# Conv weights spread by two engines, and chunk 0 quantised ahead of the expert maxima

## The reference, cut to what matters

```python
def fake_quant_nvfp4(t):              # blocks of 16 contiguous elements
    amax = jnp.max(jnp.abs(v), axis=-1, keepdims=True)
    exp = jnp.ceil(jnp.log2(jnp.maximum(amax, 1e-30) / 6.0))
    scale = jnp.where(amax > 0, jnp.exp2(exp), 1.0)
    u = v / scale
    idx = jnp.digitize(jnp.abs(u), mids)      # mids 0.25 0.75 1.25 1.75 2.5 3.5 5.0
    q = jnp.sign(u) * grid[idx]               # grid 0 0.5 1 1.5 2 3 4 6
    return (q * scale).reshape(shape)
...
x = x + conv3x3(fake_quant_nvfp4(_ln_c(x)), fake_quant_nvfp4(L0_conv_w))
t = _to_tokens(x)                     # x: (32, 64, 16, 16)
t = t + moe(_ln_t(t))                 # 8 experts 64->128->64, gelu, top-2 gates
x = _from_tokens(t, x)
```

## Time and profile before

| | us |
|---|---|
| median of 3 runs | 196.88 |
| the runs | 195.55, 196.88, 197.39 |
| profiled execution, its own time | 198.83 |
| its span in the trace | 195.9 |
| PE busy | 166.7 (85%) |
| DVE busy | 138.3 (71%) |
| POOL busy | 127.9 (65%) |
| ACT busy | 116.7 (60%) |

### The profile page before, as it was taken

How to read it: one execution, slowest core, us unless ns; L and a number is a source line. 1 busy time by engine, 2 the same in 40 slices (tenths; PEclk the granted TensorE clock), 3 DMA queues, 4 the chain that set the end, 5 groups by cost and what they waited for, 6 DMA issues and landing times.

```text
span 195.9 us, 3972 instructions
## 1 busy us (share of the span) xinstructions
PE 166.7 (85%) x1214; PEld 84.6 (43%) x1214; DVE 138.3 (71%) x442; ACT 116.7 (60%) x153; POOL 127.9 (65%) x120
## 2 busy tenths in 40 slices
PE   1986159899773697997999999999999899999980
PEld 1984125465472343542443443444443344444420
DVE  0899999999778985794684784595694395344451
ACT  3276902572488283469776767766776656776630
POOL 7699134799980442457577677577668477588482
PEclk9999859999997579999999999999999999999998
DMA  6990000000000059499089379569469559669601
GB/s 163 326 134 0 3 0 2 3 0 3 0 0 0 10 161 206 77 215 199 17 204 206 83 168 208 117 169 207 116 158 201 133 149 208 136 159 204 172 0 54
DMA packets 16320, 22.39 MB, mean 114 GB/s; under 512 B 2344, under 2 KB 8112, under 8 KB 16304
## 3 DMA queue, kind: packets, MB, share of 16 engines
q1 hardware_dynamic: 16144, 22.04, 50.3%
q10 hardware_dynamic: 160, 0.15, 0.3%
HBM read 19.82 MB, written 2.36 MB: 113 GB/s over the span
## 4 chain that ended last, share of the span: by engine, by line
PE 48%; DVE 25%; DMA 11%; ACT 7%; issue 6%; SPq 1%; POOLq 1%; ACTq 0%; DVEq 0%
PE ps L1060 23%; PE ps L1077 21%; DMA gbc<-gate_rows 6%; DVE xn L721 5%; DVE ssum L629 4%; DVE xn L641 2%; DMA gate_rows<-gateT 2%; DVE gbc L703 2%; DMA cw<-in_conv_w 2%; ACT xn L458 2%; DVE gbc L708 1%; DVE gbc L713 1%; PE ps L1016 1%; ACT hl L504 1%; DVE topi L801 1%
## 5 line engine op out<-in xcount | busy, mean ns | idle before, releaser
L411 POOL TENSOR_TENSOR x<-x,y_sb 128x512 f32 (+1 forms) x63 | 80.3, 1274 | 40.7 <-DVE y_sb L840 36.5
L557 ACT ACTIVATE work<-ps,bias_sb,w_back 128x1024 f32<-128x1024 f32 x64 | 77.0, 1204 | 37.9 <-PE ps L1060 37.7
L840 DVE SCALAR_TENSOR_TENSOR y_sb<-ps,bias_sb,gbc 128x512 f32<-128x512 f32 x64 | 47.4, 746 | 41.4 <-PE ps L1077 29.6
L1077 PE MATMUL ps<-work,w_sb 128*64 128x512 f32 x256 | 65.7, 593 | 1.0 <-DVE y_sb L840 0.9
L1060 PE MATMUL ps<-xT,w_hi 128*64 128x512 f16 x256 | 39.6, 389 | 1.1 <-ACT work L557 1.1
L1060 PE MATMUL ps<-xT,w_lo 128*64 128x512 f16 x256 | 39.3, 387 | 0.0
L1060 PEld LDWEIGHTS ps<-xT,w_hi 128*64 128x64 f16 x256 | 13.7, 111 | 33.3 <-issue 30.5
L1077 PEld LDWEIGHTS ps<-work,w_sb 128*64 128x64 f32 x256 | 17.9, 137 | 14.1 <-issue 2.1
L1060 PEld LDWEIGHTS ps<-xT,w_lo 128*64 128x64 f16 x256 | 15.0, 112 | 13.5 <-issue 1.0
L983 PE MATMUL ps<-qpad,cw_bd 128*128 128x512 bf16 x72 | 19.0, 411 | 1.7 <-POOL qpad L355 1.6
L355 POOL TENSOR_TENSOR qpad<-work,xn 128x512 bf16<-128x512 f32 (+1 forms) x8 | 10.6, 1328 | 8.7 <-DVE work L727 8.7
(11 more groups left out here) (113 smaller groups left out, 175.8 us busy)
## 6 DMA issues: line engine op xcount, KB each, us to landing
gbc<-gate_rows SPq DMA_DIRECT2D x16, 768.0 KB, 10.1
gbc<-gate_rows SPq DMA_DIRECT2D x16, 256.0 KB, 4.0
x_sb<-in_x SPq DMA_DIRECT2D x8, 256.0 KB, 5.3
out<-x SPq DMA_DIRECT2D x8, 256.0 KB, 10.4
w_raw<-in_W SPq DMA_DIRECT2D x2, 256.0 KB, 6.5
w_sb<-in_W SPq DMA_DIRECT2D x1, 256.0 KB
gate_rows<-gateT SPq DMA_DIRECT2D x8, 32.0 KB, 3.8
cw<-in_conv_w ACTq DMA_DIRECT2D x2, 72.0 KB, 3.9
```

Of the source, the lines that this page charges most:

```text
L411: pool.tensor_tensor(x2[:, ds(c * W, W)], x2[:, ds(c * W, W)], y_sb[:, u % H_RING, :], ALU.add).then_inc(added, 1)
L557: act.activation(h_sb[:, u % H_RING, :], bank(H + 2 * (u % 2), 2 * W), ACT.Gelu, bias=b1_sb[:, u:u + 1], scale=w_back[:, u:u + 1]).then_in ...
L840: dve.scalar_tensor_tensor(y_sb[:, u % H_RING, :], bank(Y + u % 2), b2_sb[:, u:u + 1], gbc[:, slot, u, :], ALU.add, ALU.mult).then_inc(wei ...
L1077: last = pe.matmul(ps[r * CH:(r + 1) * CH, (Y + u % 2) * W:(Y + u % 2 + 1) * W], w2_sb[:, u, :], h_sb[:, u % H_RING, r * W:(r + 1) * W], s ...
```

## The change

It has four parts.

- The four comparisons on POOL lose their second ALU step (a multiplication by 1.0). POOL's multiplication by the block scale goes away; DVE multiplies the sign by the block scale instead, early, behind a new link on the sign. POOL's last multiplication waits for that (`cw_signed_scale`).
- `cw_x` is written by one copy on DVE (partitions 0 to 63) and one on ACT (64 to 127), each of twice the elements, in place of four on DVE. `cw_bd` is written by ACT (0 to 63) and DVE (64 to 127), in place of two copies on ACT. DVE's copy waits for the matmuls and for ACT's `bias_ready`. ACT's absolute value of chunk 2 moves behind its normalisation of chunk 7 and its new copy.
- DVE does the conv weights and the whole of chunk 0 ahead of the maxima of the expert weights; chunk 1's maxima come behind those.
- PE's transpose of the expert maxima and the matmul that spreads them move behind convolution 0.

```diff
@@ POOL
-                last = pool.tensor_scalar(cw_steps[:, k, :], cw_a[:, :], E2M1_MIDS[k], 1.0, ALU.is_ge, ALU.mult)
+                last = pool.tensor_scalar(cw_steps[:, k, :], cw_a[:, :], E2M1_MIDS[k], None, ALU.is_ge)
...
-            link(pool.tensor_tensor(cw_steps[:, 1, :].rearrange("p (b k) -> p b k", k=BLK),
-                                    cw_steps[:, 0, :].rearrange("p (b k) -> p b k", k=BLK),
-                                    cw_scale[:, :].unsqueeze(2).to_broadcast([128, WBLK, BLK]), ALU.mult))
-            pool.tensor_tensor(cw_n[:, :], cw_steps[:, 1, :], cw_sign[:, :], ALU.mult).then_inc(cw_level_ready, 1)
+            pool.wait_ge(cw_signed_scale, 1)
+            pool.tensor_tensor(cw_n[:, :], cw_steps[:, 0, :], cw_sign[:, :], ALU.mult).then_inc(cw_level_ready, 1)
@@ ACT
             normalise(NCH - 2)
-            take_v(2)
             normalise(NCH - 1)
-            for c in range(3, NCH - 3):
+            act.wait_ge(cw_level_ready, 1)
+            act.wait_ge(cwx_zero, 1)
+            act.activation(cw_x[CH:128, :, :, 1, :], cw_n[CH:128, :].rearrange("p (i k) -> p k i", k=TAPS)
+                           .unsqueeze(2).to_broadcast([CH, TAPS, 2, HALF_IN]), ACT.Copy).then_inc(cwx_by_act, 1)
+            for c in range(2, NCH - 3):
                 take_v(c)
-            act.wait_ge(bT_ready, 1)
             act.wait_ge(cwT_ready, 1)
             act.activation(bias_sb[:, :], ps[:, BT:BT + 2 * EXPERTS], ACT.Copy).then_inc(bias_ready, 1)
-
-            act.wait_ge(cwT_ready, 1)
-            act.wait_ge(cwx_zero, 1)
-            for r in range(2):
-                lanes = slice(r * CH, (r + 1) * CH)
-                last = act.activation(cw_bd[lanes, :, r, :],
-                                      ps[lanes, CWT:CWT + TAPS * CH].rearrange("p (k o) -> p k o", k=TAPS), ACT.Copy)
-                last.then_inc(cwbd_ready, 1)
+            act.activation(cw_bd[0:CH, :, 0, :],
+                           ps[0:CH, CWT:CWT + TAPS * CH].rearrange("p (k o) -> p k o", k=TAPS),
+                           ACT.Copy).then_inc(cwbd_by_act, 1)
@@ DVE
-            dve.tensor_scalar(cw_sign[:, :].bitcast(i32), cw_u[:, :].bitcast(i32), SIGN_BIT, ONE_BITS,
-                              ALU.bitwise_and, ALU.bitwise_or)
+            link(dve.tensor_scalar(cw_sign[:, :].bitcast(i32), cw_u[:, :].bitcast(i32), SIGN_BIT, ONE_BITS,
+                                   ALU.bitwise_and, ALU.bitwise_or))
+            dve.tensor_tensor(blocks(cw_sign), blocks(cw_sign), wide(cw_scale), ALU.mult).then_inc(cw_signed_scale, 1)
...
-                for half in range(2):
-                    lanes = slice(half * CH, (half + 1) * CH)
-                    for r in range(2):
-                        last = dve.tensor_copy(cw_x[lanes, :, r, half, :],
-                                               cw_n[lanes, :].rearrange("p (i k) -> p k i", k=TAPS))
-                last.then_inc(cwx_ready, 1)
+                dve.tensor_copy(cw_x[0:CH, :, :, 0, :], cw_n[0:CH, :].rearrange("p (i k) -> p k i", k=TAPS)
+                                .unsqueeze(2).to_broadcast([CH, TAPS, 2, HALF_IN])).then_inc(cwx_by_dve, 1)
+
+            def take_conv_weights():
+
+                dve.wait_ge(cwT_ready, 1)
+                dve.wait_ge(bias_ready, 1)
+                dve.tensor_copy(cw_bd[CH:128, :, 1, :],
+                                ps[CH:128, CWT:CWT + TAPS * CH].rearrange("p (k o) -> p k o", k=TAPS)
+                                ).then_inc(cwbd_by_dve, 1)
...
             def quantise_step(c):
                 block_bounds(c)
-                if c > 0:
+                if c > 1:
                     bias(c - 1)
...
+            conv_weights()
+            block_maxima(0)
+            block_bounds(0)
+            block_magics(0)
+            magics(0)
+            bias(0)
+            take_conv_weights()
             weight_maxima()
-            block_maxima(0)
-            conv_weights()
-            quantise_step(0)
+            block_maxima(1)
             weight_exponents()
             quantise_step(1)
             weight_powers()
@@ PE
-            pe.wait_ge(xn1_ready, XN_BY_DVE)
-            pe.wait_ge(w_amax_ready, 1)
-            pe.transpose(ps[0:EXPERTS + 1, WT:WT + 128], w_amax[:, :], identf[:, :]).then_inc(w_maxT_ready, 1)
...
             for c in range(NCH):
                 convolve(c)
+                if c == 0:
+                    pe.wait_ge(xn1_ready, XN_BY_DVE)
+                    pe.wait_ge(w_amax_ready, 1)
+                    pe.transpose(ps[0:EXPERTS + 1, WT:WT + 128], w_amax[:, :], identf[:, :]).then_inc(w_maxT_ready, 1)
+                    pe.wait_ge(w_diag_ready, 1)
+                    pe.matmul(ps[:, WB:WB + EXPERTS + 1], ones_row[:, :], w_diag[:, :],
+                              start=True, stop=True).then_inc(w_spread, 1)
```

More of the change, by code:

```diff
@@ L167, in program @@
         cw_steps_ready = sem("cw_steps_ready")
+        cw_signed_scale = sem("cw_signed_scale")
         cw_level_ready = sem("cw_level_ready")
-        cwx_ready = sem("cwx_ready")
+        cwx_by_dve = sem("cwx_by_dve")
+        cwx_by_act = sem("cwx_by_act")
         cwT_ready = sem("cwT_ready")
-        cwbd_ready = sem("cwbd_ready")
+        cwbd_by_dve = sem("cwbd_by_dve")
+        cwbd_by_act = sem("cwbd_by_act")
         bT_ready = sem("bT_ready")
@@ L380, in _ @@
             pool.wait_ge(w_hi_ready, 1)
-            pool.wait_ge(cwx_ready, 1)
+            pool.wait_ge(cwx_by_dve, 1)
+            pool.wait_ge(cwx_by_act, 1)
             pool.tensor_tensor(w_scaled[:, 0:NW].rearrange("p (e h) -> p e h", e=EXPERTS),
@@ L965, in _ @@
             last.then_inc(bT_ready, 1)
-            pe.wait_ge(cwx_ready, 1)
+            pe.wait_ge(cwx_by_dve, 1)
+            pe.wait_ge(cwx_by_act, 1)
             for k in range(TAPS):
@@ L971, in _ @@
             last.then_inc(cwT_ready, 1)
[L972 to L976, removed]
+            pe.wait_ge(cwbd_by_dve, 1)
+            pe.wait_ge(cwbd_by_act, 1)
             pe.wait_ge(bias_ready, 1)
```

## The result

The changed kernel takes 201.53 us (median of 4 runs, 199.77 to 204.8) against 197.13 for the kernel before (median of 4, 195.55 to 197.92). The ratio is 1.016, interval 1.009 to 1.023, that is 3.1 us slower (1.8 to 4.5). The medians hold every run and the ratio leaves out the disturbed ones, which is why the one says 4.4 and the other 3.1. The profiled execution took 200.13 with a span of 198.3 (before: 198.83 and 195.9).

The account below looks back on a forecast made before the run. DVE, without gaps in the quantisation, was taken to bound the part before the experts. The walk gave +3.8 at chunk 7 and +4.0 at ACT's L511, taken as +3.9 on the median 196.88: 200.8 us, range 198.0 to 203.0.

Parts of the forecast that it names:

- DVE bounds the first part: Up to chunk 7's bias at 46.73, each us added to DVE or stood still there moves everything behind it.
- Part 1: POOL's cheaper levels: ready between 17.1 and 19.7, before DVE asks at 19.85, so nobody starts earlier; 0 us.
- Part 2: DVE's new multiplication of sign by block scale, beside POOL's first comparison: everything comes 0.75 later, bounds 0.50 and 1.5.
- Rival B: New multiplication on DVE blocked for POOL's whole operation: 1.5 instead of 0.75, total 201.6; chance 0.10.
- Part 3: Chunk 0 first, with one spread copy on DVE at pitch 0.62; chunk 0's bias ends at 23.0 instead of 25.54.
- Part 4: DVE idles 1.3 before its cw_bd copy, for ACT's bias_ready, and 2.35 before the exponents, for PE's transpose behind convolution 0.
- rival A: PE's clock still high at 25.1: convolution 0 takes 2.19, second wait 0.85, walk +2.2, total 199.1; chance 0.17.
- The walk: Step-by-step schedule of chunks 1 to 7: delay of +4.0 at chunk 1, +3.8 at chunk 7, +4.0 at ACT's L511.
- The rule for who waits for POOL: DVE's L708, L713 and L721 wait for a running POOL tensor operation, L721 then needs 0.55 more; others don't wait.
- Rival C: DVE's standing time paid back in the quantisation, six avoided POOL meetings giving 3.3: +0.6, 197.5; chance 0.10.
- Rival D: Convolutions and POOL's first residual set the pace, so convolution 0's 2.0 earlier start reaches the end: 194.9; chance 0.08.

Follow-up runs that it names:

- e1: Changed kernel with ACT's three absolute values (chunks 2 to 4) moved behind its copies of the biases and of cw_bd; 1.023 of the kernel before.
- e4: Kernel before with only the new levels: single-step comparisons on POOL, DVE multiplying the sign by the block scale; 1.0015 of the kernel before.
- e5: Changed kernel with expert maxima ahead of DVE's cw_bd copy, exponents right behind it, PE's transpose and spread ahead of convolution 0; 1.0005 of before.
- e2: Changed kernel with DVE's exponents behind chunk 1's quantisation step and the powers behind chunk 1's bias; 1.021 of the kernel before.
- e11: Changed kernel, ACT's absolute values behind the bias copy, POOL's residuals of chunks 0 to 4 cut to 8 columns; chunk 7's bias at 47.60.
- e9: Kernel before with POOL's residual additions of chunks 0 to 4 cut from 512 to 8 columns; chunk 7's bias at 42.79 instead of 46.73.
- e3: Changed kernel with the old levels: two-step comparisons and block scale on POOL, no sign multiplication on DVE; 203.77 us (200.18 to 206.79).
- e6: Changed kernel, expert transpose and spread before convolution 0, expert then chunk 1 maxima before exponents, both cw_bd halves on ACT; 196.98 us, 0.9946 of before.

## Why the prediction was right

It said 200.8 (198.0 to 203.0), slower; 201.53 was measured. Step by step:

- **DVE bounds the first part** (what bounds the kernel now): right up to chunk 3, where shifts of DVE were passed on to 0.01 us (0.76 in e1, 0.56 in e4, 3.30 in e5); only in e2 did a meeting with POOL's write take part of one. "Each us added to DVE moves everything behind it" is wrong from chunk 4 on: a lead of 0.76 was gone at chunk 7 (e1), one of 0.88 was down to 0.17 with residuals of 8 columns (e11), and e9 shows POOL's residuals on the path. There the moment counts at which POOL's first residual falls between two of DVE's steps.
- **Part 1, the levels, 0 us**: right as to nobody starting earlier. The four comparisons fell from 4.95 to 3.98, inside the bounds. In the changed order the levels have slack of 1.04, and putting the old ones back made the kernel's first part 0.5 shorter (e3).
- **Part 2, the multiplication, 0.75**: it cost 0.60 (19.70 against 19.10), as the operation took 0.57 where L609 takes 0.46. Rival B, the full lock, is out: the multiplication ran from 9.24 on, beside POOL's comparison from 9.07 on, and lost 0.11. The Trainium skill (SBUF — State Buffer, "Who interferes with whom") has a DVE instruction with two SBUF inputs contend with a GpSimd instruction that reads SBUF, for a lock that only one of them can hold. That agrees with the meetings of the magics with POOL's two-input operations (1.75 instead of 0.68 in e1), and not with the multiplication beside a comparison.
- **Part 3, the spread copy, pitch 0.62 within 0.42 to 0.78**: mis-sized. One copy of 64x576 took 1.16 on DVE, with the next step 1.09 behind its start, and 1.23 on ACT, where I had 0.65. On DVE that lies outside the bounds of 0.42 to 0.78. Four of 288 took 1.56, so the merged one writes half as much for three quarters of the time. The bias of chunk 0 ended at 23.34 instead of 23.0 and `bias_sb` at 24.81 instead of 24.25.
- **Part 4, the two waits, 1.3 and 2.35**: measured 1.58 and 2.11, with the releasers that were named. That their sum, 3.69, is so near the 3.65 forecast is in part luck: `bias_sb` came 0.56 late and DVE 0.34, which lengthens the first wait, while the exponents could start 0.55 late (29.70 against 29.15) and DVE asked for them 0.8 late (27.6 against 26.8), which shortens the second. The clock was low during convolution 0 (3.82 us), so rival A is out. e5 shows that the waits are most of the loss: with both filled the logits come 2.43 earlier, and without DVE's copy into `cw_bd` another 2.21. Of these 1.33 are there at chunk 1 (the copy's 0.76, e5's wait of 0.38 and a gap); 0.87 came between chunks 3 and 7, with the first residual on the other side of DVE's magics.
- **The walk**: +4.0 at chunk 1, +3.8 at chunk 7, +4.0 at ACT's L511; measured +4.55, +4.12 and +4.22. The rule for who waits for POOL held in the rows of the changed kernel but for one, and there luck helped. I had chunk 4's magics wait for the first residual (POOL at 39.27, DVE at 39.29), and POOL waited instead. So bias 3, 0.55 behind the walk (38.00 against 37.45), became a bias 4 that was 0.25 ahead of it (41.05 against 41.3). e1 took the turn as walked: from a bias 3 at 37.23 it came to 41.36, and on to bias 7 in 13.74 where the changed kernel took 12.85. With the walked turn +4.12 would have been about +5.0 by this estimate.
- **Rival C, paid back in the quantisation**: 0.43 of 4.55 was, not 3.3. **Rival D** is out: convolution 0 ended at 29.5, and DVE asked for the exponents at 27.6.

What stays open: the ratio speaks of 3.1 us and the traces ahead of the experts of 3.9 to 4.3. The expert part varies by 3 us between executions, more than that difference, and four runs don't settle it. For a profiled execution like that of the kernel before the forecast was 202.7; it took 200.13, though chunk 7's bias came 0.3 later than forecast, so the nearness of 201.53 to 200.8 says less than the steps above. Nor do the runs say why the merged copy is slow, or what the clock's phase is worth in each version.

## What to carry to other kernels

When an engine without any gap sets the pace, ask of each wait that a change gives it what stands behind the releaser: here the copy waited for ACT behind three absolute values that nobody needed yet, and the exponents for a transpose that had been put behind a convolution. With nothing waiting, the kernel with chunk 0 first had its first logits 0.3 to 0.7 us ahead of the kernel before (e6); with the waits they came some 4 us behind. Where two engines take turns, a gain of less than one turn may vanish, so measure it at the end of the stage as well as where it arises, and take a second trace of the same kernel to see what a difference there means.

## What the runs showed that I had not expected

- One strided copy of 64 partitions by 576 elements to bf16 takes 1.16 on DVE and 1.23 on ACT, against 0.65 for ACT's copy of the same size out of PSUM, which reads elements that lie side by side, and 0.39 for each of four strided copies of 288 on DVE, one behind the other. Why the merged form is slower per element was not tried.
- The order in which DVE and POOL meet decides 1.1 us at chunk 4, 0.9 at chunk 7, at a distance of 0.02 to 0.06 us (39.27 and 39.29 in the changed kernel, 38.46 and 38.52 in e1). In the changed kernel the one that started first by the trace, POOL, was the one that waited.
- After its rise between 29 and 30 us the granted clock fell back to 0.50 by 33 us, after little work on PE in between, and the transposes and the first part of convolution 1 ran at the low level again (2.78 instead of 2.19; 4.02 in e3, where all of it did).
